# The delta layer of a two-layer network: 64-column levels of a triangular inverse, and a new order of its round

## The chip, the cores and the metric

The kernel runs on one core of one Trainium2 chip. The metric is the device time of one execution in microseconds (us). The engines are named as the profile names them: PE (TensorE, with PEld for its weight loads), DVE (VectorE), ACT (ScalarE), POOL (GpSimd) and SP (SyncE, which here only issues DMAs).

## The reference

The network has four layers, each followed by a residual sum and a normalisation. Only the first, a gated delta rule with 8 batches, 1024 steps, 512 model columns and a state of 128 x 128, is touched:

```python
k = kr / jnp.maximum(jnp.linalg.norm(kr, axis=-1, keepdims=True), 1e-12)
def step(S, inp):
    q_t, k_t, v_t, a_t, b_t, g_t = inp
    Sk = jnp.einsum('bij,bj->bi', S, k_t)
    S_new = a * (S - b * (Sk[:, :, None] * k_t[:, None, :])) + b * (v_t[:, :, None] * k_t[:, None, :])
    o = jnp.einsum('bi,bij->bj', q_t, S_new) * g_t
    return (S_new, o)
...
x = _layernorm(x + o @ Wo + bo)
```

The other three layers (a quantised MLP, an attention, a low-rank MLP) stand as they were.

## The kernel before

`delta_rule_and_weights` works in chunks of 128 steps. There are 8 chunks and 2 groups of 4 batches (index s, 0 to 3), so 16 **rounds**, numbered n = 2c + g. Inside a chunk the recurrence becomes a lower triangular system of 128 rows for each batch. A round **prepares** group g of chunk c (everything that does not need the state) and in the same list of pieces **finishes** the round before (everything that does). One list of pieces, `ORDER`, is walked by every engine; each engine has its own function for a piece, in program order, and semaphores join them. The order on every engine is thus written by hand. The last round uses `ORDER_LAST`, which adds the first work for the next layer's weights (`dequant` on DVE, 12 tiles of 128x512; `la_hi`, `lb_hi` on ACT), and a list `TAIL` finishes the last round.

The pieces of a round, with PE's part first:

- `xT.s`: 4 transposes of x for batch s into a bank `p_tr` (L714); ACT copies it to `xT_hi` (L470) and seeds the bias (L465), DVE forms the remainder `xT_lo` (L565).
- `proj.s`: 12 matmuls of 512 columns (L726 to L728) for q, k, v and the gate; ACT squares and copies (L478 to L481).
- `ab`: 8 matmuls of 512 columns for alpha and beta (L739, L740); then a chain ACT `ab_low` (L486), DVE `ab_sum` (L570), ACT `ab_row` and `a_rest` (L488, L489). `decay` starts with small transposes (L751), broadcasts a_rest (L753, L754), and DVE scans it to `DT` (L579) and scales k to `kb` and `khat` (L585, L586), with the root by POOL's `pow` (L404).
- `qkT`, `kk`, `M`: transposes of q, kb, khat (L765), their product (L773), its masked negative `MnT` (DVE, L601), and its transpose (L782), copied under a mask into W[0] (L609).
- the **levels** of the inverse, i = 1 to 6, in two halves h of two batches. The block of size 2^i of the inverse follows from the one of half the size: `Y` multiplies MnT with X, 128 columns (L796); DVE copies it under the mask of the level into W[i], which else holds the identity (L615); the same X is transposed by PE (L799) and copied by ACT (L514); `X` multiplies the two (L809) and ACT copies the result (L520). The sixth level ends in `inverse` (L819).

```python
for s in (2 * h, 2 * h + 1):
    last = mm(halves[h][:, s % 2, :], MnT[:, s, :], X[:, s, :], start=True, stop=True)
last.then_inc(s_["Y_ps"], 1)
for s in (2 * h, 2 * h + 1):
    last = nc.tensor.transpose(pair[h][:, s % 2, 1, :], X[:, s, :], ident)
```

- of the round before: `KS`, `U`, `PT`, `S`, `O` (the state, fp32 matmuls of 128 columns, L828 to L869), `ogT` (4 transposes, L877; ACT and DVE split it, L646), `attn.s` (3 matmuls of 512 columns, L887 to L889), `z` (DVE adds, then the mean and the variance, L655 to L659; POOL takes the root, L422, L424) and `norm` (DVE, L665). Between KS and S, POOL adds the bias to `x_res` (L431, 4 times). SP stores x1 (L332) and loads x (L337), the residual (L340) and the weight rows of the next layer (L343).

An fp32 matmul of 128 columns, and so each of `Y` and `X`, is recorded as two matmuls ("x2" in the program is "x4" in the trace); here each of these is called a **pass**, and it has a weight load (PEld) of its own. A transpose is one pass.

## Time and profile before

| | |
|---|---|
| time, median of 3 runs | 2592.81 us (2591.26 to 2596.82) |
| time of the profiled execution | 2591.87 us |
| its span | 2589.9 us |
| mean granted clock of PE | 0.987 |
| busy: PE, PEld, DVE, ACT, POOL | 96%, 79%, 63%, 49%, 26% |
| the delta layer's rounds | from 8.87 us (first matmul on x) to 795.1 us |
| its tail, with the weights of the next layer | 795.1 to 849.0 us |

The profiled execution took 2591.87 us, 1.97 us more than its span, which starts with the first and ends with the last recorded work. A row of the timeline gives the start and the length in us, the engine, the line, the operation and what it writes and reads; "x8" merges eight. Matmul ends are modelled and overlap, so the spacing of starts is what PE needs for one.

### The profile page before, as it was taken

How to read it: one execution, taken by the hardware profiler on the slowest of the kernel's cores; microseconds unless marked ns; L12 is line 12 of the kernel's file. 1: busy time of each engine (PE TensorE's matmuls, PEld its weight loads, DVE VectorE, ACT ScalarE, POOL GpSimd, SP SyncE). 2: the span in 40 equal slices, each digit the busy share in tenths (PEclk: the TensorE clock that was granted, in tenths of full speed). 3: DMA queues.
4: the chain of work that ended last, by engine and by line, in shares of the span. 5: the costliest groups of instructions: out<-in, count | busy, mean ns of one | idle time of the engine just before them, and what ended most of it. 6: DMA issues, size and time to landing. Idle time of an engine off the chain costs nothing. (4 is left out here: it accounts for less than half of the span.)

```text
span 2589.9 us, 38373 instructions
## 1 busy us (share of the span) xinstructions
...
## 2 busy tenths in 40 slices
...
GB/s 128 49 66 35 95 65 32 97 65 32 97 113 119 1 17 82 1 98 0 33 64 16 81 0 91 6 17 80 16 81 0 51 158 98 97 97 97 119 108 65
DMA packets 100799, 166.35 MB, mean 64 GB/s; under 512 B 18372, under 2 KB 21572, under 8 KB 100612
## 3 DMA queue, kind: packets, MB, share of 16 engines
...
q14 instruction: 25, 0.20, 0.0%
...
## 5 line engine op out<-in xcount | busy, mean ns | idle before, releaser
L1156 ACT ACTIVATE quant_g_hi<-quant_bank,kept_beta,kept_gamma 128x512 fp32r<-128x512 f32 x192 | 150.6, 785 | 395.6 <-PE quant_bank L1298 395.6
L1129 POOL TENSOR_SCALAR quant_var<-quant_mv 128x1 f32<-128x1 f32 x256 | 56.9, 222 | 1002.0 <-DVE quant_mv L1200 1002.0
L1281 PE MATMUL quant_bank<-kept_W_hi,quant_h_hi 128*128 128x512 f32 x768 | 305.4, 398 | 0.3 <-DVE quant_h_lo L1189 0.3
L1282 PE MATMUL quant_bank<-kept_W_lo,quant_h_hi 128*128 128x512 f32 x768 | 303.5, 395 | 0.0
L1283 PE MATMUL quant_bank<-kept_W_hi,quant_h_lo 128*128 128x512 f32 x768 | 303.4, 395 | 0.0
L1198 DVE BATCH_NORM_STATS2 quant_stats<-quant_bank 128x6 f32<-128x512 f32 x192 | 133.9, 697 | 196.4 <-PE quant_bank L1283 196.4
L1624 DVE TENSOR_TENSOR mlp_g_lo<-mlp_p_h,mlp_g_hi 128x512 fp32r<-128x512 f32 x256 | 176.4, 689 | 113.8 <-ACT mlp_p_h L1564 113.3
L1563 ACT ACTIVATE mlp_g_hi<-mlp_p_h,mlp_b 128x512 fp32r<-128x512 f32 x256 | 177.5, 693 | 69.8 <-PE mlp_p_h L1664 62.5
L1308 PE MATMUL quant_bank<-quant_g_hi,kept_W_hi 128*128 128x512 f32 x512 | 205.2, 401 | 0.0
L1309 PE MATMUL quant_bank<-quant_g_hi,kept_W_lo 128*128 128x512 f32 x512 | 202.5, 396 | 0.0
L1310 PE MATMUL quant_bank<-quant_g_lo,kept_W_hi 128*128 128x512 f32 x512 | 202.4, 395 | 0.0
L1220 DVE TENSOR_TENSOR quant_g_lo<-quant_bank,quant_g_hi 128x512 fp32r<-128x512 f32 x192 | 130.2, 688 | 100.5 <-ACT quant_bank L1157 98.2
L1171 ACT ACTIVATE quant_bank<-kept_b_all 128x512 f32<-128x512 f32 x192 | 113.3, 603 | 133.5 <-DVE quant_y L1213 74.6
L1283 PEld LDWEIGHTS quant_bank<-kept_W_hi,quant_h_lo 128*128 128x128 f32 x768 | 144.0, 187 | 35.1
L1281 PEld LDWEIGHTS quant_bank<-kept_W_hi,quant_h_hi 128*128 128x128 f32 x768 | 144.0, 188 | 34.6 <-issue 0.5
L1282 PEld LDWEIGHTS quant_bank<-kept_W_lo,quant_h_hi 128*128 128x128 f32 x768 | 144.1, 188 | 34.1
L1564 ACT ACTIVATE mlp_p_h<-mlp_p_h,mlp_b 128x512 f32<-128x512 f32 x256 | 168.6, 659 | 0.0
L1213 DVE TENSOR_SCALAR quant_y<-quant_bank,quant_mv,quant_rstd 128x512 f32<-128x512 f32 x192 | 155.5, 810 | 17.3 <-POOL quant_rstd L1131 17.3
L1131 POOL TENSOR_TENSOR quant_rstd<-quant_var,quant_minus_half 128x1 f32<-128x1 f32 x256 | 140.8, 550 | 21.3
L1157 ACT ACTIVATE quant_bank<-quant_bank,kept_beta,kept_gamma 128x512 f32<-128x512 f32 x192 | 145.4, 757 | 0.0
L1166 ACT ACTIVATE quant_h_hi<-kept_x_in 128x512 fp32r<-128x512 f32 x128 | 81.9, 640 | 123.6 <-DVE kept_x_in L1232 99.7
L514 ACT ACTIVATE delta_XZ<-delta_p_pair 128x256 f32<-128x256 f32 x192 | 73.8, 384 | 136.6 <-PE delta_p_pair L799 136.3
...
## 6 DMA issues: line engine op xcount, KB each, us to landing
...
```

The source lines that it names most:

```text
L1156: nc.scalar.activation(g_hi[m][:, k, :], tr[k][:, :], ACT.Gelu, bias=beta[:, b, k:k + 1], scale=gamma[:, b, k:k + 1])
L1157: nc.scalar.activation(tr[k][:, :], tr[k][:, :], ACT.Gelu, bias=beta[:, b, k:k + 1], scale=gamma[:, b, k:k + 1]).then_inc(s["gelu_done"], 1)
L1213: nc.vector.tensor_scalar(y[m][:, e, :], lin_of["up", m, b, e][:, :], mv[m][:, e, 0:1], rstd[m][:, e:e + 1], ALU.subtract, ALU.mult).then_ ...
L1281: mm(out, x_hi, W_hi[2 * b][:, k, :], start=False, stop=False, skip_group_check=True)
L1282: mm(out, x_hi, W_lo[2 * b][:, k, :], start=False, stop=False, skip_group_check=True)
L1283: last = mm(out, x_lo, W_hi[2 * b][:, k, :], start=False, stop=k == KT - 1, skip_group_check=True)
L1308: mm(out, W_hi[2 * b + 1][:, k, cols], g_hi[m][:, k, :], start=k == 0, stop=False)
L1309: mm(out, W_lo[2 * b + 1][:, k, cols], g_hi[m][:, k, :], start=False, stop=False)
L1310: last = mm(out, W_hi[2 * b + 1][:, k, cols], g_lo[m][:, k, :], start=False, stop=k == KT - 1)
L1563: nc.scalar.activation(g_hi[:, at, :], p_h[at][:, :], ACT.Gelu_apprx_tanh, bias=b1[:, f:f + 1])
L1564: nc.scalar.activation(p_h[at][:, :], p_h[at][:, :], ACT.Gelu_apprx_tanh, bias=b1[:, f:f + 1]).then_inc(s_["gelu_done"], 1)
L1624: nc.vector.tensor_tensor(g_lo[:, at, :], p_h[at][:, :], as_f32(g_hi[:, at, :]), ALU.subtract).then_inc(s_["g_lo_done"], 1)
```

## The change

Levels: `Y` and `X` compute only the 64 columns that the level changes (`first` half of each pair of blocks), packed in the bank; ACT and DVE write them back in place among the 128. X starts out as the identity (a POOL copy each round), so W[0] is gone. The transpose of X is no longer made each level: it is made once (`T`), and then kept up in place by a matmul `Z` of 64 columns for levels 1 to 5. The halves of a level are interleaved. Round: `ab` moves behind `O`, `decay` in front of `proj.3`; `root`, `kh`, `kk`, `MnT`, `M`, `W0` work in halves; all four `attn` stand before the levels; `proj` starts on xT_hi alone. The statistics and the norm of x1 (two primes in the list) come one round later, and SP's stores with them.

```diff
+        kk_halves = [p[:, 0:2 * P].rearrange("p (s n) -> p s n", s=2) for p in (p_small, p_tr[0])]
...
+        def first(columns, i):
+            return of_level(columns, i)[:, :, :, 0, :]
+        def second(columns, i):
+            return of_level(columns, i)[:, :, :, 1, :]
+        def packed(bank, i):
+            return bank[:, :, 0:P // 2].rearrange("p s (n b) -> p s n b", b=2 ** i)
...
+        ORDER = order("""
+            bv.0' xT.0 xT.1 KS.0' proj.0 stats.0'' stats.1'' stats.2'' sq.0 copy.0 U.0' xT.2 proj.1 norm.0'' stats.3'' norm.1'' sq.1 copy.1 PT.0' xT.3 norm.2'' norm.3''
+            S.0' O.0' ab.0 root.0 proj.2 sq.2 copy.2 ogT.0' decay.0 kh.0
+            proj.3 sq.3 root.1 qkT.0 qkT.1 copy.3 attn.0' A.0 kh.1 kk.0 attn.1' MnT.0 qkT.2 qkT.3 qkA.0 z.0' M.0 W0.0 attn.2' z.1' kk.1 attn.3' MnT.1 M.1 W0.1
+            Y.1.0 T.0 Y.1.1 T.1 X.1.0 Z.1.0 X.1.1 z.2'
+            Y.2.0 Z.1.1 Y.2.1 X.2.0 Z.2.0 X.2.1 z.3'
+            Y.3.0 Z.2.1 Y.3.1 X.3.0 Z.3.0 X.3.1
+            Y.4.0 Z.3.1 Y.4.1 X.4.0 Z.4.0 X.4.1
+            Y.5.0 Z.4.1 Y.5.1 X.5.0 Z.5.0 X.5.1
+            Y.6.0 Z.5.1 Y.6.1 inverse.0 inverse.1""")
...
+            MORE["X", (i + 2, 1), 0] = [("la_hi", i, 0)]
...
+        MORE["kh", 1, 0] = [("bv", 0, 0)]
+        for i in range(GB):
+            MORE["X", (i + 2, 0), 0] = [("stats", i, 1)]
+            MORE["Z", (i + 2, 1), 0] = [("norm", i, 1)]
...
+            preparation((0, 0))
+            preparation((0, 1), (0, 0))
             with eng.Fori(1, CHUNKS - 1) as c:
-                preparation(c, 0, (c - 1, 1))
-                preparation(c, 1, (c, 0))
-            preparation(CHUNKS - 1, 0, (CHUNKS - 2, 1))
-            preparation(CHUNKS - 1, 1, (CHUNKS - 1, 0), ORDER_LAST)
+                preparation((c, 0), (c - 1, 1), (c - 1, 0))
+                preparation((c, 1), (c, 0), (c - 1, 1))
+            preparation((CHUNKS - 1, 0), (CHUNKS - 2, 1), (CHUNKS - 2, 0))
+            preparation((CHUNKS - 1, 1), (CHUNKS - 1, 0), (CHUNKS - 2, 1), order=ORDER_LAST)
...
+            for g in range(GROUPS):
+                load(CHUNKS - 1, g)
+            store(CHUNKS - 2, 0)
+            load_residual(CHUNKS - 1, 0)
...
             load_rows(0)
             sp.wait_ge(s_["xT_ps"], GB * (GROUPS * CHUNKS - 1))
             load_rows(1)
+            store(CHUNKS - 2, 1)
+            load_residual(CHUNKS - 1, 1)
             sp.wait_ge(s_["xT_ps"], GB * GROUPS * CHUNKS)
             load_rows(2)
             sp.wait_ge(s_["proj_ps"], GB * GROUPS * CHUNKS)
             load_rows(3)
...
+            def root(c, g, h):
+                n = GROUPS * c + g
+                half = slice(2 * h, 2 * h + 2)
+                pool.wait_ge(s_["floor_done"], 2 * n + h + 1)
+                nc.gpsimd.tensor_tensor(rn[:, half], ss_floor[:, half], minus_half[:, half], ALU.pow).then_inc(s_["rn_done"], 1)
...
+                    nc.gpsimd.tensor_copy(XZ[g][:, :, 0, :], ident4[:, :, :]).then_inc(s_["x_ident"], 1)
...
+            def Y(c, g, at):
+                i, h = at
+                wait_apart(dve, s_["Y_ps"], 2 * ((LEVELS - 1) * (GROUPS * c + g) + i - 1) + h + 1, settled)
+                nc.vector.copy_predicated(first(W[i][:, 2 * h:2 * h + 2, :], i), first(mask[:, i:i + 1, :], i).to_broadcast([P, 2, P // 2 >> i, 1 << i]),
+                                          packed(halves[h], i)).then_inc(s_["W_done"], 1)
...
+                    nc.vector.tensor_copy(XZ[g][:, 2 * h:2 * h + 2, 1, :], kk_halves[h]).then_inc(s_["Z0_done"], 1)
...
+                    nc.vector.tensor_copy(second(XZ[g][:, 2 * h:2 * h + 2, 1, :], i), packed(kk_halves[h], i)).then_inc(s_["Z0_done"], 1)
...
-                pe.wait_ge(s_["xT_lo_done"], GB * n + s + 1)
+                pe.wait_ge(s_["xT_hi_done"], GB * n + s + 1)
...
                     mm(out, xT_hi[:, s, k, :], w_lo[:, k, cols], start=False, stop=False, skip_group_check=True)
+                pe.wait_ge(s_["xT_lo_done"], GB * n + s + 1)
+                for k in range(KT):
...
+            def kk(c, g, h):
+                n = GROUPS * c + g
+                pe.wait_ge(s_["qkT_done"], GB * n + 2 * h + 2)
+                for s in (2 * h, 2 * h + 1):
+                    last = mm(kk_halves[h][:, s % 2, :], qkT[g][:, s, 2, :], qkT[g][:, s, 1, :], start=True, stop=True)
                 last.then_inc(s_["kk_ps"], 1)
...
-            def Y(c, g, i):
+            def Y(c, g, at):
+                i, h = at
                 n = GROUPS * c + g
                 if i == 1:
-                    pe.wait_ge(s_["W0_done"], n + 1)
-                    wait(pe, s_["S_done"], GB * n)
-                for h in range(2):
-                    if i > 1:
-                        pe.wait_ge(s_["X_done"], 2 * ((LEVELS - 2) * n + i - 2) + h + 1)
-                    X = W[0] if i == 1 else XZ[g][:, :, 0, :]
-                    for s in (2 * h, 2 * h + 1):
-                        last = mm(halves[h][:, s % 2, :], MnT[:, s, :], X[:, s, :], start=True, stop=True)
-                    last.then_inc(s_["Y_ps"], 1)
-                    for s in (2 * h, 2 * h + 1):
-                        last = nc.tensor.transpose(pair[h][:, s % 2, 1, :], X[:, s, :], ident)
-                    last.then_inc(s_["Z_ps"], 1)
...
+                    if h == 0:
+                        wait(pe, s_["S_done"], GB * n)
+                    pe.wait_ge(s_["W0_done"], 2 * n + h + 1)
+                else:
+                    pe.wait_ge(s_["X_done"], 2 * ((LEVELS - 2) * n + i - 2) + h + 1)
+                two = slice(2 * h, 2 * h + 2)
+                X, out = first(XZ[g][:, two, 0, :], i), packed(halves[h], i)
+                for s in range(2):
+                    last = mm(out[:, s], MnT[:, 2 * h + s, :], X[:, s], start=True, stop=True)
+                last.then_inc(s_["Y_ps"], 1)
+            def T(c, g, h):
+                for s in range(2):
+                    last = nc.tensor.transpose(kk_halves[h][:, s, :], XZ[g][:, 2 * h + s, 0, :], ident)
+                last.then_inc(s_["Z_ps"], 1)
+            def X(c, g, at):
+                i, h = at
+                e = (LEVELS - 1) * (GROUPS * c + g) + i
+                pe.wait_ge(s_["Z1_done" if h else "Z0_done"], e)
+                pe.wait_ge(s_["W_done"], 2 * e - 1 + h)
+                two = slice(2 * h, 2 * h + 2)
+                W_first, out = first(W[i][:, two, :], i), packed(pair[h][:, :, 0, :], i)
+                for s in range(2):
+                    last = mm(out[:, s], XZ[g][:, 2 * h + s, 1, :], W_first[:, s], start=True, stop=True)
+                last.then_inc(s_["X_ps"], 1)
+            def Z(c, g, at):
+                i, h = at
+                two = slice(2 * h, 2 * h + 2)
+                Z_second, out = second(XZ[g][:, two, 1, :], i), packed(kk_halves[h], i)
+                for s in range(2):
+                    last = mm(out[:, s], W[i][:, 2 * h + s, :], Z_second[:, s], start=True, stop=True)
+                last.then_inc(s_["Z_ps"], 1)
+            def inverse(c, g, h):
+                e = (LEVELS - 1) * (GROUPS * c + g) + LEVELS - 1
+                pe.wait_ge(s_["Z1_done" if h else "Z0_done"], e)
+                pe.wait_ge(s_["W_done"], 2 * e - 1 + h)
+                two = slice(2 * h, 2 * h + 2)
+                Z_second, out = second(XZ[g][:, two, 1, :], LEVELS - 1), packed(pair[h][:, :, 0, :], LEVELS - 1)
+                for s in range(2):
+                    last = mm(out[:, s], W[LEVELS - 1][:, 2 * h + s, :], Z_second[:, s], start=True, stop=True)
+                last.then_inc(s_["inverse_ps"], 1)
...
-                if not isinstance(n, int) or n < GROUPS * CHUNKS - 1:
-                    pe.wait_ge(s_["ab_done"], n + 2)
...
+                elif not isinstance(n, int) or n < GROUPS * CHUNKS - 1:
+                    pe.wait_ge(s_["proj_done"], GB * n + GB + s + 3)
```

On PE, in the fourth level of a round (the prediction's term for the levels rests on it), before:

```order
L796 MATMUL delta_p_wide<-delta_XZ_112,delta_MnT 128x128 x2
L799 MATMUL delta_p_pair<-kept_ident_61,delta_XZ_112 128x128 x2
L796 MATMUL delta_p_tr<-delta_XZ_112,delta_MnT 128x128 x2
L799 MATMUL delta_p_pair<-kept_ident_61,delta_XZ_112 128x128 x2
L809 MATMUL delta_p_pair<-delta_W_83,delta_XZ_112 128x128 x4
```

and now, for a level of the changed program (from `Y.2.0` to `X.2.1`):

```order
L890 MATMUL delta_p_wide<-delta_XZ_76,delta_MnT 128x64 x2
L917 MATMUL delta_p_tr<-delta_XZ_76,delta_W_80 128x64 x2
L886 REGISTER_ALU
L890 MATMUL delta_p_tr<-delta_XZ_76,delta_MnT 128x64 x2
L903 REGISTER_ALU
L904 ISA
L908 MATMUL delta_p_pair<-delta_W_81,delta_XZ_76 128x64 x2
L917 MATMUL delta_p_small<-delta_XZ_76,delta_W_81 128x64 x2
L908 MATMUL delta_p_pair<-delta_W_81,delta_XZ_76 128x64 x2
```

Four transposes became four fp32 matmuls (L917), and every matmul has 64 columns in place of 128.

On DVE, at the start of a round, before (L565 xT_lo, L623 bR, L628 wU):

```order
L565 TENSOR_TENSOR delta_xT_lo<-delta_p_tr,delta_xT_hi 128x512
L564 REGISTER_ALU
L565 TENSOR_TENSOR delta_xT_lo<-delta_p_tr,delta_xT_hi 128x512
L621 ISA
L622 REGISTER_ALU
L623 TENSOR_TENSOR delta_bR<-delta_bv_102,delta_p_wide 128x512
L628 TENSOR_TENSOR delta_wU<-delta_p_pair,delta_DT_103 128x512
```

and now, from bR on:

```order
L707 TENSOR_TENSOR delta_bR<-delta_bv_102,delta_p_wide 128x512
L743 ISA
L744 BN_STATS delta_stats<-delta_z 128x6
L746 BN_AGGR delta_mv<-delta_stats 128x2
L743 REGISTER_ALU
L744 BN_STATS delta_stats<-delta_z 128x6
L746 BN_AGGR delta_mv<-delta_stats 128x2
L743 REGISTER_ALU
L744 BN_STATS delta_stats<-delta_z 128x6
L746 BN_AGGR delta_mv<-delta_stats 128x2
L712 TENSOR_TENSOR delta_wU<-delta_p_pair,delta_DT_103 128x512
```

The statistics moved from the levels to between bR and wU, and the four norms follow among xT_lo, PT and og. On SP, behind its loop, the change sets (140 to 143 are the rows of weight layers 0 to 3):

```order
L358 DMA x_d<-delta_z 128x4x512
L365 DMA delta_x_res_96<-L_attn_x_d 128x4x512
L379 DMA delta_rows_140<-L_ffn_qweights_d 128x4x512
L379 DMA delta_rows_141<-L_ffn_qweights_d 128x4x512
L358 DMA x_d<-delta_z 128x4x512
L365 DMA delta_x_res_121<-L_attn_x_d 128x4x512
L379 DMA delta_rows_142<-L_ffn_qweights_d 128x4x512
L379 DMA delta_rows_143<-L_ffn_qweights_d 128x4x512
```

The rows of layer 2 now stand behind the store of round 13, which waits for a norm that is made inside the last round; before, both stores stood ahead of the first rows.

## Rows read from the trace of the kernel before

**Rows 1.** Windows: length, busy of PE, PEld, DVE, ACT, POOL; clock, DMA share, GB/s.

```profile
402.00:451.00 49.00, 46.67 (x309) 39.42 (x309) 27.96 (x53) 22.03 (x58) 13.13 (x17) 1.00 0.13 43
39.00:46.00 7.00, 3.93 (x16) 2.52 (x14) 4.29 (x7) 2.45 (x7) 1.22 (x2) 0.76 0.01 2
```

**Rows 2.** Timeline of PE: the first transposes of rounds 1 and 9.

```profile
65.17 1.04 PE L714 MATMUL delta_p_tr<-kept_ident,delta_x_in 128*128 128x128 f32 x8
...
454.22 1.04 PE L714 MATMUL delta_p_tr<-kept_ident,delta_x_in 128*128 128x128 f32 x8
```

**Rows 3.** Timeline of PE in round 8: spacing of passes and 512-column matmuls.

```profile
410.27 0.40 PE L728 MATMUL delta_p_pj<-delta_w_hi,delta_xT_lo 128*128 128x512 f32 x1
410.50 1.06 PE L837 MATMUL delta_p_pair<-delta_XZ,delta_bR 128*128 128x128 f32 x8
411.40 1.06 PE L840 MATMUL delta_p_pair<-delta_bR,delta_XZ 128*128 128x128 f32 x8
```

**Rows 4.** Timeline of PE in round 8: from proj.3 to the levels.

```profile
426.14 0.40 PE L751 MATMUL delta_p_small<-kept_ident,delta_ab_row 2*128 2x2 f32 x4
...
427.56 1.16 PE L857 MATMUL delta_p_small<-delta_S,delta_qkA 128*128 128x128 f32 x8
...
430.27 0.32 PE L765 MATMUL delta_p_tr<-kept_ident,delta_qkv 128*128 128x128 f32 x1 [0.66 <-DVE delta_khat L586]
...
434.68 0.50 PE L887 MATMUL delta_p_pj<-delta_wo_hi,delta_ogT_hi 128*128 128x512 f32 x1 [0.61 <-DVE delta_ogT_lo L646]
...
436.97 0.71 PE L796 MATMUL delta_p_wide<-delta_W,delta_MnT 128*128 128x128 f32 x4 [0.19 <-DVE delta_W L609]
```

**Rows 5.** Timeline of PE in round 8: the fourth level.

```profile
445.96 0.71 PE L796 MATMUL delta_p_wide<-delta_XZ,delta_MnT 128*128 128x128 f32 x4
...
448.58 0.68 PE L796 MATMUL delta_p_wide<-delta_XZ,delta_MnT 128*128 128x128 f32 x4
```

**Rows 6.** Timeline of PEld: two weight loads after a wait.

```profile
434.68 0.19 PEld L887 LDWEIGHTS delta_p_pj<-delta_wo_hi,delta_ogT_hi 128*128 128x128 f32 x1 [0.80 <-DVE delta_ogT_lo L646]
434.79 0.19 PEld L888 LDWEIGHTS delta_p_pj<-delta_wo_lo,delta_ogT_hi 128*128 128x128 f32 x1
```

**Rows 7.** Groups, 65 to 746 us: count, busy us, mean ns, idle before.

```profile
L615 DVE COPY_PREDICATED delta_W<-delta_mask,delta_p_wide 128x256 f32<-128x256 int32 x84 | 37.6, 447 | 17.5 <-PE delta_p_wide L796 16.1
...
L579 DVE TENSOR_TENSOR_SCAN delta_DT<-delta_p_wide,kept_ident 128x512 f32<-128x512 f32 x14 | 17.0, 1212 | 0.0
...
L586 DVE TENSOR_TENSOR delta_khat<-delta_qkv,delta_rn 128x512 f32<-128x512 f32 x14 | 9.6, 683 | 0.0
...
L520 ACT ACTIVATE delta_XZ<-delta_p_pair 128x256 f32<-128x256 f32 x140 | 53.8, 384 | 43.8 <-PE delta_p_pair L809 37.4
...
L478 ACT ACTIVATE delta_sq<-delta_p_pj 128x128 f32<-128x128 f32 x56 | 15.6, 278 | 84.6 <-PE delta_p_pj L728 83.0
```

**Rows 8.** Timeline of ACT in round 8: the chain from ab to a_rest.

```profile
420.68 0.59 ACT L486 ACTIVATE delta_ab_low<-delta_p_small 2x512 f32<-2x512 f32 x1 [2.56 <-PE delta_p_small L740]
...
422.64 0.70 ACT L489 ACTIVATE delta_a_rest<-delta_ab_sum,delta_b_ab 2x508 f32<-2x508 f32 x1
```

**Rows 9.** Timeline of DVE in round 8: two norms, one beside POOL's residual.

```profile
449.40 0.55 DVE L665 TENSOR_SCALAR delta_z<-delta_z,delta_mv,delta_rstd 128x512 f32<-128x512 f32 x1
...
450.73 1.42 DVE L665 TENSOR_SCALAR delta_z<-delta_z,delta_mv,delta_rstd 128x512 f32<-128x512 f32 x1
```

**Rows 10.** Timeline of PE in round 0.

```profile
42.48 0.48 PE L765 MATMUL delta_p_tr<-kept_ident,delta_qkv 128*128 128x128 f32 x1 [2.57 <-DVE delta_khat L586]
42.75 0.42 PE L765 MATMUL delta_p_tr<-kept_ident,delta_kb 128*128 128x128 f32 x1
...
49.60 0.71 PE L796 MATMUL delta_p_wide<-delta_W,delta_MnT 128*128 128x128 f32 x4 [0.92 <-DVE delta_W L609]
```

**Rows 11.** Timeline of SP and DVE about the start of round 15.

```profile
744.16 0.40 SPq L332 DMA_DIRECT2D x_d<-delta_z  x1
...
754.92 1.90 DVE L678 SCALAR_TENSOR_TENSOR delta_rows<-delta_rows,delta_scale 128x512 f32<-128x512 int32 x3 [4.81 <-DMA delta_rows<-L_ffn_qweights_d]
```

More of the change, by code:

```diff
@@ L242, in delta_rule_and_weights, with order @@
-        for i in range(2, LEVELS):
-            ORDER += [("Y", i, False)]
-            ORDER += [("attn", i, True)] * (i < GB) + [("z", i - 1, True)] * (i - 1 < GB) + [("norm", i - 2, True)] * (i - 2 < GB)
-            ORDER += [("X" if i < LEVELS - 1 else "inverse", i, False)]
+        def order(text):
+            pieces = []
+            for word in text.split():
+                what, *i = word.rstrip("'").split(".")
+                i = tuple(int(v) for v in i)
+                pieces.append((what, i if len(i) > 1 else i[0], word.count("'")))
+            return pieces
@@ L434, in _ @@
             pool.wait_ge(s_["bo_in"], 16)
[L435 removed]
+            run(pool, {"KS": residual(0), "U": residual(1), "PT": residual(2), "S": residual(3), "xT": identity, "root": root, "kh": kh, "qkA": qkA_, "stats": stats_})
         @block.scalar
```

240 lines of the change are left out of this document (120 added, 120 removed).

## The prediction

> **What bounds the kernel now.** I read the windows first: in 402 to 451 us, one round, PE is busy 46.67 of 49 us at full clock, DVE 28 and ACT 22 [rows 1]. Modelled ends hide short waits, so I count starts instead. Rounds begin with the first transposes of x: eight rounds take 454.22 - 65.17 = 389.05 us, 48.63 each [rows 2]. A pass with 128 columns takes (411.40 - 410.50)/8 = 0.112 us, a 512-column matmul 0.23 [rows 3]. By the code a round has 228 passes (xT 16, KS 8, U 16, PT 8, S 16, O 16, qkT 12, ogT 4, kk 8, M 4, levels 6 x 20 = 120), 68 matmuls of 512 columns, and decay, 427.56 - 426.14 = 1.42 [rows 4]: 25.5 + 15.6 + 1.4 = 42.6 us of work. So PE waits 6.0 us in each round. Where: from decay to the levels (426.14 to 436.97, 10.83 us) the work is 1.42 + 44 x 0.112 + 6 x 0.23 = 7.7, the waits 3.1. The three waits shown there are for khat, ogT_lo and W[0], each a DVE result of 512 columns that depends on all four batches [rows 4]. In the levels (436.97 to 454.22, 17.25 us) the work is 120 x 0.112 + 6 x 0.23 = 14.8, the waits 2.4 [rows 2, 4]; a level without attn takes 2.62 us against 20 x 0.112 = 2.24 [rows 5]. The first 20.5 us hold 0.5 of waits. The kernel is bound by PE's work, and second by the chains of a round.
>
> **The levels: fewer columns, not less time.** The decisive price is that of a pass with 64 columns, which the trace doesn't have. It streams half, but loads 128 columns of weights as before. The row: after a wait, two loads start at 434.68 and 434.79 [rows 6], though the 512-column matmuls that they serve take 0.23 each [rows 3]. So two full loads follow each other in 0.11 us with nothing but themselves to hold the second, and 0.11 is a pass. Lower end: 0.105, as far as the rounding of that spacing allows; upper end 0.13, if load and stream are not quite hidden. Four transposes that stream 2 columns take at most 0.40/4 = 0.10 each [rows 4], so a short stream adds little to a load. I take 0.112: the 64 columns give PE nothing. And the levels get more passes: Y 48, X 40, inverse 8, T 4, and Z 40 where 24 transposes were: 140 instead of 120, **+2.2 us a round**.
>
> The Trainium skill puts this into a rule (TensorE: Matmul & The Clock Gate, section LDWEIGHTS): a load takes its column count over 1.2 GHz, whatever is streamed. That is 107 ns for 128 columns, the trace's two loads being 110 apart; by the page's figure the 136 short passes would take 0.7 us a round less than in my sum.
>
> **What the interleaving buys.** With 24 passes a level lasts 2.69 us at least. Counted from the start of X.i.0 (PE then does Z.i.0, X.i.1, Y.i+1.0, Z.i.1, Y.i+1.1, 0.45 each): its last pass starts at 0.34 and is over some 0.25 later, ACT copies 128 columns in 0.28 [rows 7], done by 0.9, and Y.i+1.0 is due at 1.35. Y is over at 1.9, DVE's masked copy of 128 columns costs under the 0.45 of 256 [rows 7], done by 2.4, and X.i+1.0 is due at 2.69. Every link has 0.3 us to spare, so the 2.4 us of waits shrink to about 0.3. DVE's z is gone from all but two levels, its statistics and norms from all. The levels: 15.7 + 0.3 = 16.0, before 17.25 - 1.38 = 15.9. **No gain there.**
>
> **The middle.** The rest is in halves, with independent work between:
> - ab to decay. From the start of ab_low to the end of a_rest the chain takes 422.64 + 0.70 - 420.68 = 2.7 us [rows 8], and ab_low starts about 0.2 after ab's last matmul. Before, two proj (24 x 0.23 = 5.5 us) covered it; now proj.2 (2.8) and ogT (0.45). It just fits: wait 0.1.
> - decay to qkT.0. DVE must do a_first, the scan (1.21) and half of kb and khat (half of 0.68 each) [rows 7], 2.2 us, partly behind ogT_lo; proj.3 (2.8) covers them but for 0.1. The wait for khat (0.66 [rows 4]) goes.
> - qkT.0, qkT.1, attn.0, then kk.0 for ACT's second copy of qkT: 0.2. attn.1 for the copy of proj.3, behind those: 0.2. attn.3 for z.1, behind W0.0 on DVE: 0.15. A load laid bare after each: 0.2 in all. X.1.0 for DVE's copy of T: 0.1.
> Sum 1.05, where 3.1 were. In the first 20.5 us, proj.0 no longer waits for xT_lo (0.2 of the 0.5 goes). What DVE gets there, 4 statistics and 4 norms (0.55, or 1.42 where POOL's residual runs beside [rows 9]), lies between its own work, xT_lo, bR, wU, PT, og and S; a statistics piece is one 512-column read and a short one, which I put at 1 us from the 0.68 of khat [rows 7]. Together 6 to 10 us beside 8 of its own, in the 17 us before ab_sum is due: it fits, with 0 to 2 us to spare. POOL's identity copy and halved pows lie in its idle time. Waits after: 1.05 + 0.3 + 0.3 = 1.6.
>
> A round after: 42.6 + 2.2 + 1.6 = 46.4 us, against 48.6. **Rounds 1 to 14: 14 x -2.25 = -31.5 us.**
>
> **Round 0** finishes nothing, so its chains lie open: PE waits 2.57 us for khat and 0.92 for W[0] [rows 10]. With decay ahead of proj.3 the first goes (qkT.0 follows proj.3), and the halves save about 1: **-4 us**.
>
> **Round 15.** DVE has 12 dequants of 1.90/3 = 0.63 us besides [rows 11], and now the statistics and norms of round 13 on top in the first 17 us; ab_sum comes 2 us late. Worse, the rows of weight layer 2 stand on SP behind the store of round 13, which waits for that round's last norm, some 17 us into the round, and behind a residual load. Before, a store began at 744.16, residual and rows followed, and the first tile of rows was there at 754.92 [rows 11]: 10.8 us with 4 transfers of 1 MB under way; with 3, about 8. So in the round's own time dequant (2,0) starts at 25 to 26, then four of them (2.5), ogT_lo (0.7), the scan (1.2) and half of kb and khat (0.7): qkT.0 at about 30.7, where by the sums above it is due at 24. PE stands for 5 to 7 us. After such a stretch its granted clock can be at the lower level: in 39 to 46 us, behind the wait of 2.57, the window shows 0.76 of full, and a pass is recorded with 0.42 us, which is 1.2 GHz against the 2.4 GHz of the rounds after [rows 1, 10]; that is 1 us more. Against the 2.25 gained like any round: **+5 us** (0 if the transfer is in time, +10 if it is late and the tail inherits it). The tail has the same pieces: 0.
>
> **Sum:** -31.5 - 4 + 5 = -30.5 on the profiled execution's 2591.9 us: 2561.4. The median of the runs stands 0.9 above that execution: 2562. I say 2562.
>
> **Rivals.**
> 1. *The middle keeps its waits* (20%): DVE is in order, and z.0, W0.0, z.1, MnT.1 and kh.1 stand in one queue; if each link is 0.2 late, 1.4 us come back in each round: 2562 + 19.6, 2581. For: rows 4 are all waits for DVE. Against: every piece is half as long.
> 2. *The load doesn't count* (5%): a short pass costs its stream, half of 0.112. Then levels are bound by the chain Y, copy, X, copy (0.45 from the first pass to the read of the bank, twice; 0.37 and 0.34 for the copies: 1.6 us), 9.7 instead of 16: 6.3 us a round, 2562 - 95 = 2467. Against: rows 6. The Trainium skill (same page, section Back-to-back issue gap) gives the isolated gap as columns over 2.4 GHz plus 2.5 ns, by which the time would fall so; the same section says that a stream of loads and matmuls is set by both.
> 3. *The load adds to the stream* (9%, **slower**): a short pass and the next load don't overlap, so that a pass costs both: 0.11 + 0.056 = 0.166. The place is the 136 short passes, the price 136 x 0.054 = 7.3 us a round, +110 in 15: 2672. It decides from 30.5/15/136 = 0.015 us a pass on: at 0.127 the gain is gone. For: the first Y pass after a wait takes longer by its bare load, 436.97's four lasting 0.71 [rows 4]. Against: with 128 columns eight passes with eight loads take 0.90 [rows 3], so load and stream do overlap.
> 4. *No change* (5%): the moved statistics and norms, with every norm at 1.42 [rows 9], make DVE 2 us late for ab_sum in each round, and decay waits as long; 30 us, about 2592. Against: only the norms that meet one of POOL's four residual pieces can be long.
>
> **How the numbers follow.** The forecast has 61%. Its own range: 0.105 a pass and 0.5 us fewer waits give -17 more (2545), 1 us more of waits and +5 in round 15 give +20 (2582). To hold the time 8 times in 10 it reaches to rival 1 and toward 4: 2538 to 2588. Faster by over 0.2% (5 us; about what a measurement of this kernel can tell from none): 0.61 + 0.20 + 0.05 = 0.86; the same 0.05; slower 0.09.
>
> **What would show it.** Right: starts of 64-column passes 0.11 apart, levels of 2.7 us, rounds of 46.4, no wait on khat over 0.3. The levels' share of the round unchanged. A wait of PE of 5 us or more before qkT in round 15, ended by DVE, itself held by the rows' DMA. Wrong: passes 0.06 or 0.16 apart; PE waiting for a_rest in every round (DVE too full in the first part); a level over 2.8.

## The result, and the profile after

The changed kernel takes 2567.03 us (median of 4 runs, 2565.83 to 2568.26), the kernel before 2592.23 (4 runs): 25.2 us less, ratio 0.990 with a 95% interval of 0.988 to 0.992. The forecast was 2562, so it was 5 us too low. The profiled execution has a span of 2565.9 us against 2589.9, 24.0 less.

Windows of the changed kernel: the 49 us of [rows 1], and all of rounds 1 to 14 (length, busy of PE, PEld, DVE, ACT, POOL; clock, DMA share, GB/s).

```profile
402.00:451.00 49.00, 48.89 (x337) 42.23 (x336) 30.49 (x68) 18.41 (x53) 12.93 (x18) 1.00 0.18 60
...
61.61:711.74 650.13, 648.52 (x4538) 568.41 (x4538) 388.67 (x856) 249.49 (x728) 173.86 (x241) 1.00 0.20 66
```

PE now has 337 records in the window where it had 309, is busy all the time, and ACT does less. The starts of rounds, 61.61 for round 1 and 711.74 for round 15, give (711.74 - 61.61)/14 = 46.44 us a round; before it was 48.63 [rows 2].

PE's timeline around the fifth level of round 8, which answers to [rows 5]:

```profile
428.03 0.61 PE L890 MATMUL delta_p_wide<-delta_XZ,delta_MnT 128*128 128x64 f32 x4
428.47 0.61 PE L917 MATMUL delta_p_tr<-delta_XZ,delta_W 128*128 128x64 f32 x4
428.92 0.61 PE L890 MATMUL delta_p_tr<-delta_XZ,delta_MnT 128*128 128x64 f32 x4
429.37 0.61 PE L908 MATMUL delta_p_pair<-delta_W,delta_XZ 128*128 128x64 f32 x4
429.81 0.61 PE L917 MATMUL delta_p_small<-delta_XZ,delta_W 128*128 128x64 f32 x4
430.26 0.61 PE L908 MATMUL delta_p_pair<-delta_W,delta_XZ 128*128 128x64 f32 x4
430.71 0.61 PE L890 MATMUL delta_p_wide<-delta_XZ,delta_MnT 128*128 128x64 f32 x4
```

Each group of four passes starts 0.447 us behind the one before: 0.112 a pass, the price of a pass with 128 columns [rows 3], and a level is 430.71 - 428.03 = 2.68 us without a gap. From the first Y (417.11) to the next round (433.23) the levels last 16.12 us.

The groups of the levels' copies, 61 to 712 us (count, busy us, mean ns, idle before), which answer to L615 and L520 in [rows 7]:

```profile
L578 ACT ACTIVATE delta_XZ<-delta_p_pair 128x128 f32<-128x128 f32 x140 | 39.1, 279 | 78.7 <-PE delta_p_pair L908 77.4
...
L686 DVE COPY_PREDICATED delta_W<-delta_mask,delta_p_wide 128x128 f32<-128x128 int32 x84 | 27.2, 324 | 30.2 <-PE delta_p_wide L890 28.1
```

PE's timeline in the middle of round 8, where [rows 4] had its waits:

```profile
406.63 0.41 PE L839 MATMUL delta_p_tr<-kept_ident,delta_ab_row 2*128 2x2 f32 x4
...
410.94 0.27 PE L856 MATMUL delta_p_tr<-kept_ident,delta_qkv 128*128 128x128 f32 x1
...
412.39 0.71 PE L864 MATMUL delta_p_small<-delta_qkT 128*128 128x128 f32 x4
...
417.11 0.56 PE L890 MATMUL delta_p_wide<-delta_XZ,delta_MnT 128*128 128x64 f32 x4
```

Decay starts 19.88 us into the round (386.75), the first Y 10.48 later. Between them stand decay (1.42), 24 x 0.112 = 2.7 and 24 matmuls of 512 columns (5.6): 9.7, so 0.8 us of waits. No row of this stretch has a bracket.

The last round is the bad place. PE, DVE and SP of the changed kernel:

```profile
745.53 0.47 PE L856 MATMUL delta_p_tr<-kept_ident,delta_qkv 128*128 128x128 f32 x1 [5.49 <-DVE delta_khat L651]
...
769.30 1.09 PE L928 MATMUL delta_p_pair<-delta_XZ,delta_W 128*128 128x64 f32 x4 [0.92 <-DVE delta_W L686]
```

```profile
725.22 3.65 DVE L765 SCALAR_TENSOR_TENSOR delta_rows<-delta_rows,delta_scale 128x512 f32<-128x512 int32 x3
...
731.87 0.67 DVE L628 TENSOR_TENSOR delta_ab_sum<-delta_p_tr,delta_ab_low 2x512 f32<-2x512 f32 x1
...
740.46 2.50 DVE L765 SCALAR_TENSOR_TENSOR delta_rows<-delta_rows,delta_scale 128x512 f32<-128x512 int32 x4 [6.71 <-DMA delta_rows<-L_ffn_qweights_d]
```

```profile
729.82 0.39 SPq L358 DMA_DIRECT2D x_d<-delta_z  x1
...
730.80 9.64 SPq L379 DMA_DIRECT2D delta_rows<-L_ffn_qweights_d  x2
```

SP issues the rows of weight layer 2 at 730.80, 19.1 us into the round; DVE waits 6.71 us for them, and PE 5.49 for khat behind DVE. PE waits another 2.4 us for a_rest, since ab_sum starts at 731.87, 20.1 into the round, where round 8 has it at 17.4. Of both delays 1.8 us have one source: the three dequants from 725.22 on take 3.65 us, where the three before them (at 715.82) took 1.89, and ab_sum, the last two norms and the store behind these stand in line behind them. POOL adds the bias to x_res beside them (724.75 to 727.72); that this slows them is read from the rows, no run separates it.

Where the 24 us come from, by starts of PE:

| | before | after | difference |
|---|---|---|---|
| round 0 | 56.30 | 52.90 | -3.4 |
| rounds 1 to 14 | 680.91 | 650.13 | -30.8 |
| round 15, to the tail's first matmul (L828, L937) | 49.00 | 58.44 | +9.4 |
| tail, to the next layer's first 512-column matmul | 56.14 | 56.77 | +0.6 |

The first matmul on x stands 0.16 us earlier, and 0.3 us are lost behind the tail: -24.0 in all.

### The profile page after: what moved, and what is told of

It is laid out like the page before. It is cut to its first block and busy times, and to the rows that moved or that the text cites. A ratio compares the mean times of both kernels' runs of the same rounds, so it can differ in the third digit from the quotient of the medians.

```text
span 2565.9 us, 39230 instructions
## 1 busy us (share of the span) xinstructions
PE 2479.4 (97%) x13400; PEld 2065.4 (80%) x13400; DVE 1642.0 (64%) x3012; ACT 1194.1 (47%) x2321; POOL 669.0 (26%) x1074
## 5 line engine op out<-in xcount | busy, mean ns | idle before, releaser
L1322 DVE TENSOR_SCALAR quant_y<-quant_bank,quant_mv,quant_rstd 128x512 f32<-128x512 f32 x192 | 155.5, 810 | 17.4 <-POOL quant_rstd L1240 17.1
L1628 POOL TENSOR_SCALAR mlp_z<-mlp_z,mlp_mv,mlp_rstd 128x512 f32<-128x512 f32 x60 | 123.8, 2076 | 0.0
```

What stands on the lines that cost most here:

```text
L1322: nc.vector.tensor_scalar(y[m][:, e, :], lin_of["up", m, b, e][:, :], mv[m][:, e, 0:1], rstd[m][:, e:e + 1], ALU.subtract, ALU.mult).then_ ...
```

## The experiments

Differences are against the changed kernel's 2567.03 us unless another kernel is named. The kernel before, run beside each group of experiments, took 2592.45 to 2593.76 us (2592.23 beside the changed kernel), so a difference of under 2 us in the time alone is not told from none; the lengths of rounds are averages over rounds 1 to 14 of one profile each. Moving `ab` behind `O`, and all four `attn` ahead of the levels, has no run of its own.

### Streamed columns (e1), loaded columns (e2)

```diff
 # PE, Y (X, Z and inverse likewise)
-X, out = first(XZ[g][:, two, 0, :], i), packed(halves[h], i)
+X, out = XZ[g][:, two, 0, :], halves[h]
 # DVE reads of the bank (ACT likewise)
-packed(halves[h], i)
+first(halves[h], i)
```

> The changed kernel, but Y, X, Z and the inverse stream all 128 columns of the block; DVE and ACT still copy only the 64 that change. Same passes, same loads, same copies. Load-bound theory (a pass costs its load of 128 columns, 0.112 us): the spacing of four passes stays 0.4475 us, rounds stay 46.44, 2567 within 3 us. Rival, the stream counts in part (the 64 columns save something a pass, if little): every 0.005 us a pass on 136 passes is 0.68 us a round, +10 us; a saving of a quarter of the stream (0.013) would show as +28 us.

Measured: 2570.53 us (2570.28 to 2570.96), +3.5, just over the 3 allowed. Rounds last 46.56 us, 0.12 more. PE's timeline shows the same spacing with twice the columns:

```profile
420.54 0.61 PE L908 MATMUL delta_p_pair<-delta_W,delta_XZ 128*128 128x128 f32 x4
420.99 0.61 PE L890 MATMUL delta_p_wide<-delta_XZ,delta_MnT 128*128 128x128 f32 x4
421.43 0.61 PE L917 MATMUL delta_p_tr<-delta_XZ,delta_W 128*128 128x128 f32 x4
```

So streaming 64 columns saves PE nothing inside a chain of passes: 0.112 us either way. The 0.12 us a round lies at least in part at groups that start after a wait: Y.1.1 and X.1.0 last 0.55 and 0.54 us until the next group, where the changed kernel has 0.50 and 0.49.

The next edit narrows the weights (it leaves out half of the rows of Y, so its results are not those of the layer):

```diff
-last = mm(out[:, s], MnT[:, 2 * h + s, :], X[:, s], start=True, stop=True)
+last = mm(out[0:P // 2, s], MnT[:, 2 * h + s, 0:P // 2], X[:, s], start=True, stop=True)
```

> The changed kernel, but Y loads only 64 of the 128 columns of MnT as weights, so that half of the rows of Y are left out (48 of the 136 short passes load and stream 64). Load-bound theory: these passes cost 0.056 us instead of 0.112, 48 x 0.056 = 2.7 us a round less work; the chains Y, copy, X, copy have 0.3 us to spare a link now and would eat up to 1 us of it: -25 to -43 us, about 2530. Rival, a fixed price of 0.11 us per pass whatever is loaded or streamed (issue, or the two-part fp32 form): spacing stays 0.4475, 2567 within 3 us.

Measured: 2576.88 us (2572.95 to 2577.74), **+9.8**; rounds of 47.00. Neither theory. PE's timeline of a level:

```profile
428.41 0.61 PE L908 MATMUL delta_p_pair<-delta_W,delta_XZ 128*128 128x64 f32 x4
428.95 0.45 PE L890 MATMUL delta_p_wide<-delta_XZ,delta_MnT 128*64 128x64 f32 x4
429.33 0.66 PE L917 MATMUL delta_p_tr<-delta_XZ,delta_W 128*128 128x64 f32 x4
429.92 0.45 PE L890 MATMUL delta_p_tr<-delta_XZ,delta_MnT 128*64 128x64 f32 x4
```

The narrow group gives 0.07 us (429.33 - 428.95 = 0.38 for 0.45), but the group ahead of it lasts 0.54 (428.41 to 428.95) or 0.59 (429.33 to 429.92) instead of 0.45: 0.09 and 0.14 us are lost at the change from wide to narrow weights, once for each half in a level; a whole level lasts 2.82 us where the changed kernel has 2.68. Late data are not the reason: from X.0 to the next Y.0 there are 1.48 us (430.29 to 431.77), and in e3 below 1.02 are enough. A narrow load is recorded with 136 ns, a wide one with 192. The price of a pass is thus smaller with fewer weight columns, as I thought, but in groups of four between wide ones it brought nothing. What in the change of width costs the time, the run doesn't tell.

### Fewer passes (e3), and whole copies on top (e5)

```diff
-            Y.4.0 Z.3.1 Y.4.1 X.4.0 Z.4.0 X.4.1
+            Y.4.0 Z.3.0 Y.4.1 Z.3.1 X.4.0 X.4.1
...
 # PE, Z
-    last = mm(out[:, s], W[i][:, 2 * h + s, :], Z_second[:, s], start=True, stop=True)
+    last = nc.tensor.transpose(kk_halves[h][:, s, :], XZ[g][:, 2 * h + s, 0, :], ident)
 # DVE and ACT read second(kk_halves[h], i); POOL's identity waits for Z_ps
```

> The changed kernel, but the transpose of X is made anew by 4 transposes per level (20 passes a level, as before the change) instead of 8 passes of the matmul Z; everything else stays, 64-column Y and X, copies of 64 columns. Theory (passes are the price, the chains have room): 20 x 0.112 = 2.24 us a round less; from the first pass of X.0 to the start of Y.0 the data need 0.34 + 0.25 + 0.28 = 0.87 us and are due at 0.90, and DVE's copy of the transposed X is ready about 0.1 us before X.0 is due, so at most 0.2 us of waits a level: 1.2 to 2.2 us a round, -19 to -36 us, 2531 to 2548, levels of 2.25 to 2.45 us. Rival (Z was needed as cover: with 20 passes the waits of the old kernel, 0.4 us a level, come back): within 5 us of 2567, levels of 2.65.

Measured: 2541.28 us (2539.84 to 2543.31), **-25.8**. Rounds last 44.83 us. A level on PE:

```profile
408.00 0.66 PE L890 MATMUL delta_p_wide<-delta_XZ,delta_MnT 128*128 128x64 f32 x4
408.50 0.39 PE L915 MATMUL delta_p_small<-kept_ident,delta_XZ 128*128 128x128 f32 x2
408.73 0.56 PE L890 MATMUL delta_p_tr<-delta_XZ,delta_MnT 128*128 128x64 f32 x4
409.12 0.39 PE L915 MATMUL delta_p_tr<-kept_ident,delta_XZ 128*128 128x128 f32 x2
409.39 1.14 PE L908 MATMUL delta_p_pair<-delta_W,delta_XZ 128*128 128x64 f32 x8
410.41 0.66 PE L890 MATMUL delta_p_wide<-delta_XZ,delta_MnT 128*128 128x64 f32 x4
```

2.41 us against 2.68, and 20 x 0.112 = 2.24 of it is work. The step from X (409.39) to Y (410.41) is 1.02 where eight passes take 0.90: Y waits about 0.1 us for ACT's copy, and 0.05 each goes at T and at X. The theory holds in its middle: 1.60 of 2.24 us a round come through. The edit also puts the pieces of a level in a plain order, which e8 below has with Z still a matmul. Against e8 (2574.52 us, rounds of 47.01) the transposes alone bring 33 us, 2.18 of 2.24 us a round. With whole blocks computed and copied:

```diff
 # the kernel of e3, and
-X, out = first(XZ[g][:, two, 0, :], i), packed(halves[h], i)
+X, out = XZ[g][:, two, 0, :], halves[h]
-nc.scalar.activation(first(XZ[g][:, 2 * h:2 * h + 2, 0, :], i), packed(pair[h][:, :, 0, :], i), ACT.Copy)
+nc.scalar.activation(XZ[g][:, 2 * h:2 * h + 2, 0, :], pair[h][:, :, 0, :], ACT.Copy)
 # every copy of DVE and ACT in the levels likewise
```

> The kernel of e3 (transposes in place of Z, new order of pieces), with Y, X and the inverse on all 128 columns and DVE and ACT copying whole blocks of 256 columns: the levels' work is that of the kernel before, in the changed kernel's order. Theory (no pass gets cheaper by 64 columns; they only shorten the copies): in e3 a level is 2.41 us against 20 x 0.112 = 2.24, so the chain Y, copy, X, copy is already just bare; ACT's copy grows from 0.29 to 0.38 and DVE's masked copy from 0.29 to 0.45, of which 0.1 to 0.25 us a level comes into the open: 0.5 to 1.2 us a round over e3, 2541 + 8 to 19, about 2553, and still faster than the changed kernel's 2567. Rival A (copies hidden): 2541 within 4. Rival B (whole copies are what made the old levels wait 0.4 us): 2565 or more.

Measured: 2576.71 us (2576.58 to 2577.43), +35.4 over e3: rival B; my theory's 8 to 19 was half of it or less. Rounds last 47.24 us. The level on PE, and DVE's copies in it:

```profile
428.40 0.71 PE L889 MATMUL delta_p_wide<-delta_XZ,delta_MnT 128*128 128x128 f32 x4
...
429.62 0.38 PE L914 MATMUL delta_p_tr<-kept_ident,delta_XZ 128*128 128x128 f32 x2
430.11 1.15 PE L907 MATMUL delta_p_pair<-delta_W,delta_XZ 128*128 128x128 f32 x8
431.29 0.71 PE L889 MATMUL delta_p_wide<-delta_XZ,delta_MnT 128*128 128x128 f32 x4
```

```profile
429.22 0.44 DVE L686 COPY_PREDICATED delta_W<-delta_mask,delta_p_wide 128x256 f32<-128x256 int32 x1 [1.20 <-PE delta_p_wide L889]
429.56 0.42 DVE L699 COPY delta_XZ<-delta_p_small 128x256 f32<-128x256 f32 x1
```

A level is 2.89 us. DVE makes both copies of half 0 one after the other, over at 429.98, and X starts at 430.11 where the transposes end at 429.84; ACT's copies are 0.1 longer each and stand in the same circle. Five levels of 0.48 more make the 2.4 us a round. Step by step around the circle, from the timelines of both kernels (DVE's first copy starts at 429.22, in e3's level at 408.77; ACT's copy of X.0 at 430.85 and 410.08): Y's start to DVE's first copy 0.82 us (e3: 0.77), from there to X 0.89 (0.62), X's start to ACT's copy 0.74 (0.69), from there to the next Y 0.44 (0.33). So 0.38 of the 0.48 are copies and 0.10 is the longer stream, which shows here because PE waits for its end. The 64 columns do bring something: 2.4 us a round once the passes are only 20, four fifths of it by shorter copies on DVE and ACT. (This is not the old level word for word: before, both transposes were copied by ACT, and attn stood between.) The runs thus split the change: from 48.64 us a round to e5's 47.24 by the new order with whole blocks, to e3's 44.83 by 64 columns, and back up to 46.44 by Z with its interleaved order.

### The interleaving (e8)

```diff
-            Y.4.0 Z.3.1 Y.4.1 X.4.0 Z.4.0 X.4.1
+            Y.4.0 Z.3.0 Y.4.1 Z.3.1 X.4.0 X.4.1
```

> The changed kernel, but the halves of a level are no longer interleaved: Y.0 Z.0 Y.1 Z.1 X.0 X.1, all 24 passes as they are. Theory of the prediction (interleaving shrinks the levels' waits from 2.4 us a round to 0.3): at least 1.5 us a round comes back, +22 or more, 2589 or more. Rival (24 passes are cover enough in either order: from X.0's first pass the data for Y.0 need 0.87 us and are due at 0.90): 0 to 0.1 us a level, 2567 to 2574.

Measured: 2574.52 us (2573.98 to 2577.88), +7.5, at the upper end of the rival; rounds of 47.01. Levels are 2.81 us: X to Y takes 1.03 where eight passes take 0.90. The interleaving is worth 0.57 us a round, not the 2.1 that I gave it. The four more passes are hardly cover either: a level waits 0.12 us here and 0.17 in e3, which has the same order and 20 passes. The old waits (0.38 a level) went mostly with the shorter copies, as e5 beside e3 shows; what the passes cover beside whole copies no run tells.

### The middle (e7, e12) and the start on xT_hi (e11)

```diff
-            S.0' O.0' ab.0 root.0 proj.2 sq.2 copy.2 ogT.0' decay.0 kh.0
-            proj.3 sq.3 root.1 qkT.0 qkT.1
+            S.0' O.0' ab.0 root.0 proj.2 sq.2 copy.2 ogT.0' proj.3 sq.3 decay.0 kh.0
+            root.1 qkT.0 qkT.1
```

> The changed kernel, but decay (and the first half of kb and khat on DVE) stands behind proj.3 again, as before the change. Theory (the middle's gain of about 2 us a round is cover: proj.3, 2.8 us, hides scan and khat): after decay DVE needs 0.16 + 1.22 + 0.40 + 0.42 us and two handovers before qkT.0, 2.2 to 2.6 us that PE now waits in each of 16 rounds, with a share given back where other waits go: +28 to +40, 2595 to 2607. Rival (halving kb and khat is what removed the wait; order counts for little): the old wait of 0.7 us, +8 to +12, about 2577.

Measured: 2636.81 us (2633.26 to 2641.29), **+69.8**, nearly twice the theory. The wait itself is as forecast; what follows it is not:

```profile
404.33 0.32 PE L856 MATMUL delta_p_tr<-kept_ident,delta_qkv 128*128 128x128 f32 x1 [2.11 <-DVE delta_khat L651]
...
405.28 0.44 PE L997 MATMUL delta_p_pj<-delta_wo_lo,delta_ogT_hi 128*128 128x512 f32 x1
405.51 0.63 PE L998 MATMUL delta_p_pj<-delta_wo_hi,delta_ogT_lo 128*128 128x512 f32 x1
...
408.56 0.42 PE L856 MATMUL delta_p_tr<-kept_ident,delta_khat 128*128 128x128 f32 x1
...
408.95 0.27 PE L856 MATMUL delta_p_tr<-kept_ident,delta_kb 128*128 128x128 f32 x1
```

From 405.5 to 408.9 a 512-column matmul is recorded with 0.63 us instead of 0.40 and a pass with 0.42 instead of 0.27: PE runs at 1.2 GHz. The windows give the granted clock: 0.78 in 404.3 to 412, 1.00 in 412 to 428. Over rounds 1 to 14 a round lasts (779.18 - 77.96)/14 = 50.09 us, 3.65 more for a wait of 2.1. The rounds are of two kinds: the slow stretch behind the wait lasts 3.4 us as here, and the round 49.4 to 49.8, or 6.8 us (rounds 5, 8, 11 and 14), and the round 50.9 to 51.0; round 1, 50.8, has the short one and starts at the low clock. Round 0 takes 69.43 instead of 52.90: from 40.6 us, behind a wait of 2.0 for khat, to its end PE stays at a clock of 0.50, through all six levels. What makes a stretch long or short, these rows don't tell. Rounds 1 to 14 lose 51 us by this, round 0 16.5. The old waits of 0.6 and 0.7 us had left the clock at 1.00 [rows 1, 4].

The staggering of the halves undone:

```diff
-attn.0' A.0 kh.1 kk.0 attn.1' MnT.0 qkT.2 qkT.3 qkA.0 z.0' M.0 W0.0 attn.2' z.1' kk.1 attn.3' MnT.1 M.1 W0.1
+attn.0' A.0 kh.1 attn.1' qkT.2 qkT.3 qkA.0 z.0' attn.2' kk.0 kk.1 z.1' attn.3' MnT.0 MnT.1 M.0 M.1 W0.0 W0.1
```

> The changed kernel, but the two halves of kk, MnT, M and W0 stand back to back behind the last qkT (attn.1, qkT.2, qkT.3, attn.2, kk.0, kk.1, attn.3, MnT, M, W0), so that their chain is that of all four batches again. Theory of the prediction (the middle's gain is the staggering of halves): attn.3 (0.7 us) covers z.1 or MnT on DVE but not both, M.0 waits 0.3 to 0.6 us, Y.1.0 waits for W0.0 another 0.5 to 0.7: +0.8 to +1.3 us a round, +13 to +21, 2580 to 2588, and with waits under 1 us no fall of PE's clock in steady rounds. Rival (decay ahead of proj.3 alone did it, the halves add nothing): within 4 of 2567.

Measured: 2580.22 us (median of 10 runs), +13.2; seven runs take 2579 to 2581, three 2595, and the profiled one is of the three. From round 4 on its rounds last 47.3 us, +0.9: the theory's size. Its waits from 61 to 712 us, where 13 rounds have theirs (us in total, times, longest):

```profile
PE delta_p_wide L890 <- DVE delta_XZ L680: 7.1, 13, 0.8
PE delta_p_pj L996 <- ACT delta_gate L533: 6.4, 13, 0.6
```

The wait for W0.0 (L890) is the theory's, the other is not: instead of M.0, attn.1 (L996) waits 0.5 us, for ACT's copy of proj.3, which kk.0 had covered.

The 15 us between its runs are most likely in round 0: in the profiled one it lasts 66.0 us, 13.1 more than in the changed kernel, and its windows show PE busy with a clock of 0.56 and then 0.50 up to 75 us, as in e7:

```profile
40.00:61.00 21.00, 19.61 (x95) 18.76 (x95) 5.98 (x17) 3.75 (x13) 7.96 (x7) 0.56 0.00 1
61.00:75.00 14.00, 14.00 (x67) 14.00 (x67) 2.96 (x9) 2.37 (x9) 0.00 (x0) 0.50 0.01 2
```

In the changed kernel's profile 40 to 61 us has 1.00. The profile is of a long run, so that the shorter ones lack this stretch is not shown. The last edit of this group:

```diff
-                pe.wait_ge(s_["xT_hi_done"], GB * n + s + 1)
+                pe.wait_ge(s_["xT_lo_done"], GB * n + s + 1)
```

> The changed kernel, but each proj waits for xT_lo before its first matmul, as before the change. Theory of the prediction: about 0.2 us a round comes back, at proj.0: +2 to +4, 2570. Rival (DVE now has statistics and norms in front of xT_lo, so that the wait is longer than the old one and proj.2 and proj.3 meet it too): 0.5 us a round or more, 2575 or more.

Measured: 2569.06 us (2568.89 to 2569.97), +2.0; a round is 0.15 us longer, all at proj.0. As forecast.

### Round 15 (e6, e4)

```diff
-            store(CHUNKS - 2, 1)
-            load_residual(CHUNKS - 1, 1)
             sp.wait_ge(s_["xT_ps"], GB * GROUPS * CHUNKS)
             load_rows(2)
+            store(CHUNKS - 2, 1)
+            load_residual(CHUNKS - 1, 1)
```

> The changed kernel, but SP issues the weight rows of layer 2 ahead of the store of round 13 and the residual load, so as soon as the last x is transposed. Theory (round 15 is long because these rows start late): they start 14 us into the round in place of 19, are there about 4 us earlier, PE's wait for khat falls from 5.5 to 1 or 2 us, and PE's clock drops for less time: -4 to -5, 2562. Rival (DVE's own queue, statistics, norms and 12 dequants, makes khat late): -1 or less, 2566 to 2567.

Measured: 2561.80 us (2559.16 to 2562.49), -5.2. PE's waits in round 15 no longer hold khat at all; those that stay are

```profile
PE delta_p_tr L839 <- ACT delta_a_rest L541: 2.4, 1, 2.4
...
PE delta_p_pair L928 <- DVE delta_W L686: 0.9, 1, 0.9
```

The rows are now issued at 721.85, 11.3 us into the round, earlier still than the 14 expected. Round 15 lasts 53.32 us, 5.1 less. The other way to the same end is to make the norms a round earlier:

```diff
-proj.0 stats.0'' stats.1'' stats.2'' sq.0 copy.0 U.0' xT.2 proj.1 norm.0'' stats.3'' norm.1'' sq.1
+proj.0 sq.0 copy.0 U.0' xT.2 proj.1 sq.1
...
-            Y.4.0 Z.3.1 Y.4.1 X.4.0 Z.4.0 X.4.1
+            Y.4.0 Z.3.1 norm.1' Y.4.1 X.4.0 stats.2' Z.4.0 X.4.1
...
 # SP: store and residual of round 13 ahead of load_rows(0)
```

> The changed kernel, but statistics and norms of x1 are made in the levels of the same round (one prime instead of two), SP stores a round earlier and both stores stand ahead of the weight rows of layer 1. Theory: in round 15 of the changed kernel the levels already held these very pieces and were gapless (2.68 us each), so steady rounds stay at 46.44; round 15 loses its late rows: PE's waits of 2.4 us (a_rest) and 5.5 us (khat) and the low clock behind them go: -7 to -10 us, 2557 to 2560. Rival A (DVE in the levels makes X wait, 0.1 to 0.2 us a level): +0.5 to 1 us a round, +7 to +15, net 2567 to 2574. Rival B (round 15 is late for the transfer's own length, not for its start): -2, 2565.

Measured: 2562.18 us (2561.82 to 2562.70), -4.9. Rounds 1 to 14 last 46.58 on average, +0.14; round 15 lasts 52.2, 6.3 less. Between the theory and rival A. The edit puts both stores ahead of all rows, not only of layer 1's as the expectation has it, so that even those of layer 0 come late: DVE stands 6.41 us for them near the start of the round, and PE 2.6 for wU. That this is what is missing to the 7 to 10 fits these waits; no run shows it alone. Making the norms a round later, one part of the change, thus gained 2 us in rounds 1 to 14 (14 x 0.14) and lost 6.3 or more in round 15.

### A version that beats both (e9), and a simpler one (e10)

The kernel of e3, in which round 14 makes the statistics and norms of two rounds (round 12's in its first part, as now, and round 13's in its levels) and round 15 none in its first part:

```diff
+        NORMS = {}
+        for i in range(GB):
+            NORMS["X", (i + 2, 0), 0] = [("stats", i, 1)]
+            NORMS["Z", (i + 2, 1), 0] = [("norm", i, 1)]
+        ORDER_14, ORDER_LAST = [], []
         for piece in ORDER:
-            ORDER_LAST += [piece] + MORE.get(piece, [])
+            ORDER_14 += [piece] + NORMS.get(piece, [])
+            if piece[0] not in ("stats", "norm"):
+                ORDER_LAST += [piece] + NORMS.get(piece, []) + MORE.get(piece, [])
```

> The kernel of e3 (transposes in place of Z), and round 14 also makes the statistics and norms of round 13, in its levels, so that round 15 has none of them in its first part and SP's store of round 13 no longer holds the weight rows of layer 2. Theory (late rows and the full DVE are what round 15 loses): e3's waits in round 15, 2.4 us for a_rest and 3.9 us for khat, and the low clock behind them, go; in round 14 DVE has 2.3 us of work in levels of 2.4, so up to 1 us is given back: 2541 - 5 to -8, 2533 to 2536. Rival (the waits move into the tail, where PE in e3 already waited for DVE's W_lo): 2538 to 2541.

Measured: **2529.10 us** (5 runs, 2527.90 to 2531.47), ratio to the kernel before 0.976 with a 95% interval of 0.974 to 0.977, 38 us under the changed kernel and 12.2 under e3, where I had expected 5 to 8. Round 15 lasts 45.1 us (e3: 55.3), with PE at full clock:

```profile
686.00:731.00 45.00, 44.65 (x306) 38.04 (x304) 37.59 (x77) 21.48 (x59) 13.58 (x19) 1.00 0.43 120
```

That is 10.2 us of the 12.4 between the two profiles. The rival is out: the tail (57.5 us, e3: 57.7) is not longer. Another 1.8 us lie behind it: from the next layer's first 512-column matmul to the end e3 takes 1741.9 us and e9 1740.1, although both start there at the slow level (matmuls of 0.78 and 0.63 us). Why, the rows that I read don't tell. My 5 to 8 were too low: round 15 got back nearly all that it had over a steady round (10.2 of 55.3 - 44.8).

The simpler one is the kernel of e3 with the edit of e6:

> The kernel of e3 with the order of e6 on SP (weight rows of layer 2 ahead of the store of round 13). Theory: the gain of e6 (5 us) comes on top of e3's, since the one is in round 15 and the other in every round: 2536, and behind e9 by the 2.4 us wait for a_rest that stays: 2535 to 2538. Rival (rounds are 1.6 us shorter, the transfer is not, so less of it is hidden and less gained): 2538 to 2541.

Measured: 2533.89 us (2531.98 to 2534.94), -7.4 against e3, a little more than the forecast: the two gains add, and the rival is out. It stays 4.8 behind e9; the wait for a_rest, 2.5 us in its profile, is about half of that. In the profiles its round 15 is 3.9 us longer (49.0 against 45.1).

## Why the prediction was right, and where it was off

- **A pass of 64 columns costs 0.112 us**: right (0.1118 between groups; e1: the same with 128). The levels' 20 more passes cost what was said. The Trainium skill's figure (TensorE: Matmul & The Clock Gate, section LDWEIGHTS: 107 ns for a load of 128 columns) agrees in kind, the measured spacing is 5 ns over it. Rivals 2 (half the price) and 3 (load plus stream, 0.166) fall with the same row.
- **Levels 15.9 to 16.0**: measured 16.12. The size is right, its reason only in part: the step "What the interleaving buys" put 2.1 us on the order of the halves; e8 puts 0.57 there, e5 beside e3 shows shorter copies as the larger part, and the cover of four more passes counts for little (e3 beside e8). The shorter copies stand in the prediction's chain, but not as what removes the waits.
- **Middle, waits 3.1 to 1.05**: about 0.8 with the last link counted in the levels; right. e7 and e12 show both halves of the reason: proj.3 as cover for scan and khat, and the staggered halves for 0.9 us a round.
- **First part, waits 0.5 to 0.3**: 19.88 us with 19.6 of work; e11 gives 0.15 a round for the start on xT_hi.
- **Round**: 46.44 measured, 46.4 forecast; rounds 1 to 14 -30.8 against -31.5. Rival 1 (1.4 us a round given back) and rival 4 (DVE late for ab_sum in each round; in round 8 it starts at 404.15 with 0.22 us of its own wait before it) are out.
- **Round 0**: -3.4 against -4, in part by luck. Ahead of the levels 3.9 us went, 0.5 came in the levels. The four waits behind decay fell from 4.85 us (2.57, 0.58, 0.78, 0.92) to 2.21 (0.63, 0.64, 0.42, 0.52), 2.6 less where the prediction had 3.6. The other 1.3 went with the clock: before, the first transposes behind the wait for khat ran at 1.2 GHz (0.76 in 39 to 46 us [rows 1, 10]), now 40 to 61 us has 1.00. The prediction has no term for that here.
- **Round 15, +5**: this term was mis-sized. It measured +9.4. The chain was named rightly, and e6 shows it: with the rows on time 5.2 us go. Its pieces were too small. The rows were issued 19.1 us into the round instead of 17 to 18 and took 9.7 us (730.80 to 740.46) instead of 8, so that qkT.0 began at 33.8 instead of 30.7: 3.1 of the 4.4 us. The late issue is the slow dequants', which the prediction put at 0.63 us each. The norm of 1.41 us beside POOL's residual held the inverse for 0.92, which I had left out. The low clock cost the rest: 1.3 us in place of the 1 forecast (from qkT.0 on round 15 is 2.4 us longer than round 8, 1.1 of it at the inverse), with a clock of 0.55 granted from 745.5 to 749.2 us. The late ab_sum, "2 us late" in the prediction, is PE's wait of 2.4 us for a_rest; here it ends ahead of the wait for khat and is hidden by it, in e6 it lies open.
- **Tail, 0**: +0.6, its clock being lower in the first transposes of the next layer.

Of -30.5 forecast for the span, -24.0 came: 4.4 us are missing in round 15, 0.7 in rounds 1 to 14, 0.6 each in round 0 and in the tail. The time lies in the range. One sum of the prediction doesn't come out: its own lower end, -17, should be -22 by the terms given (15 x (136 x 0.007 + 0.5)); nothing else rests on it.
